# Router rows of the last mixture of experts in the padding of its shared chunks, its top-2 weights turned in 32x32 blocks on VectorE, the last norm by tiles

## The chip, the cores and the metric

The kernel runs on one core of a Trainium2 chip. Its five engines work side by side, each through its own list of instructions: TensorE (PE; PEld are its weight loads), VectorE (DVE), ScalarE (ACT), GpSimd (POOL) and SyncE (SP), which issues nearly all transfers. The metric is device time in microseconds.

## The reference

A decoder of six residual layers, each followed by a layer norm, on 1024 tokens of 256 values in float32. The first, second, third and fifth layers matter little here; the fourth (`_L1_attn_ref`) and the sixth (`_L1_ffn_ref`) are those around the change:

```python
def _L1_ffn_ref(hidden_states, gate_weight, gate_up_weights, down_weights, shared_gate_up, shared_down):
    ...
    logits = x @ gate_weight.T
    scores = jax.nn.softmax(logits, axis=-1)
    topk_w, topk_idx = jax.lax.top_k(scores, TOP_K)
    combine = jnp.zeros((T, E), x.dtype).at[jnp.arange(T)[:, None], topk_idx].add(topk_w)
    gu = jnp.einsum('th,efh->tef', x, gate_up_weights)
    act = jax.nn.silu(gu[..., :F]) * gu[..., F:]
    y = jnp.einsum('tef,te,ehf->th', act, combine, down_weights)
    sgu = x @ shared_gate_up.T
    sact = jax.nn.silu(sgu[:, :Fs]) * sgu[:, Fs:]
    y = y + sact @ shared_down.T
```
```python
    x = _layernorm(x + _L0_attn_ref(...))
    x = _layernorm(x + _L0_xattn_ref(...))
    x = _layernorm(x + _L0_ffn_ref(...))
    x = _layernorm(x + _L1_attn_ref(...))
    x = _layernorm(x + _L1_xattn_ref(x, ctx_2048, mask_BxS2_bk0))
    x = _layernorm(x + _L1_ffn_ref(...))
```

There are E = 8 experts of F = 176 rows, TOP_K = 2, and a shared expert of 352 rows.

## The kernel before

The tokens lie in eight tiles of 128, in two halves of four tiles (`HT` = 4, T0 = 0 or 4). All weights come as packs that SP loads; a pack is split into a high part (ACT) and a low part (POOL, the difference), and a product of float32 is three PE products of these parts. Feed-forward work runs in chunks s: a gate product (`g`s), an up product (`u`s), silu (`s`, ACT), their product `hraw` (`m`, DVE), its high part (`h`, ACT) and low part (`l`, POOL), and a down product (`d`, which counts packs u). The sixth layer, f1, has 14 chunks per half: 3 with the 352 shared rows padded to 384, and 11 with the experts' rows. Half 0 has the chunks 40 to 53, half 1 the chunks 54 to 67. In routed chunks DVE multiplies by the token weights (`o`), which must have been spread over the partitions.

The order of the work of each engine is written out by hand in five lists (lines 136 to 187): `SP_ORDER`, `PE_ORDER`, `ACT_ORDER`, `POOL_ORDER`, `DVE_ORDER`. An engine takes its steps in that order, whatever is ready; semaphores keep the engines in step. Names that one step has on several engines stand for parts of one thing: `G19` is a load on SP, a high part on ACT and a low part on POOL. `G16` is the first pack of f1, so `G19` belongs to the chunk of `g43`. `D`s are the down halves of packs, `S`j the four packs of the cross-attention layer (`S4` the last, split by ACT at line 1302 and by POOL at 1531). `a0.x` and `a1.x` are steps of the fourth layer's attention of half 0 and 1, with the router of f1 among them (22 to 24) although they are written as one family: for f1 of half 0 they are `a0.22` (PE `route`, line 909: 16 matmuls; DVE logits; ACT exp), `a0.23` (DVE softmax and top 2) and `a0.24` (PE four transposes, line 1075; ACT copies the weights to `cwT`, line 1380). `a1.3` and `a1.4` are queries and keys of the fourth layer's second half, `a1.5` and `a1.6` its values, `a1.7` and `a1.8` its scores (POOL subtracts the maximum there). `e`b.x are steps of the cross-attention by example, with norms before and after it (`e2.10` to `e3.12` is the norm ahead of a1). `P0` to `P3` and `Q0` to `Q3` are the token scatters and gathers of the second layer (indirect transfers, issued by POOL, lines 1461 and 1467). `w`, `x`, `y`, `z` close f1 and the last norm.

SP's list around f1 reads `... D15 R1 G16 G17 G18 G19 G20 G21 W0 C3 C4 S4 G22 C5 G23 ...`. `W0` waits until `cwT` is done, then writes it to memory; `C`k reads rows of it back, spread over the partitions, once that has landed:

```python
            def save_weights(h):
                sp.wait_ge(sems["cwT_done"], h + 1)
                sp.dma_start(cw_dram[h, :, :], cwT[0:E1, :]).then_inc(sems["cw_saved"], 16)
```

ACT's list has there `h42 S4 G19 D19 G20 D20 G21 s43`, POOL's `l42 S4 G19 D19 G20 a1.7 a1.8 l43`, PE's `a1.5 a1.6 a1.7 g43 a1.8`. `g43` waits for G19's low part (line 557 has the first matmul of a gate).

At the end, PE runs `e44 e45 e46 f44 e47 f45 f46 f47`: `e` adds the last down products to tiles 4 and 5, `f` to tiles 6 and 7. DVE's `w0` and `w1` add them to the residual by pairs of tiles and take the statistics, POOL the power, ACT (and DVE for one tile) applies the norm, SP stores by pairs.

Of the kernel before, what the change touches and what calls it, by code (L numbers as in the profile page):

```python
# [192 lines left out]
def decoder_program(nc, x_rows, x_cols, ids, pad_mask, w_attn0, w_attn1, bias_cols, bias_rows, bias_v1, bias_o,  # L193
                    w_route, temperature, consts, pk_x0, pk_f0, pk_x1, pk_f1, cw_dram, xs_dram, ys_dram, out):
    with ExitStack() as ctx:
# [344 lines left out]
        def _(pe):  # L540
# [321 lines left out]
            def down(u, tiles=range(HT)):  # L862
# [17 lines left out]
                for t in tiles:  # L880
                    o = bank[4 + t // 2][:, (t % 2) * D:(t % 2 + 1) * D]
                    if 1 <= u < U_F1 and t % 2 == 0:
                        pe.wait_ge(sems["acc_done"], 4 * u - 2 + t)
# [145 lines left out]
            def attention(i, h):  # L1029
# [38 lines left out]
                elif i == 22:  # L1068
                    route(8 + h, 1, 2 + h)
                elif i == 24:  # L1070
                    pe.wait_ge(sems["rt_cw"], h + 1)
                    if h == 0:
                        wait_x(5)
                    for t in range(HT):
# [1211 lines left out]
```

## Time and profile before

| | us |
|---|---|
| median of 3 runs | 424.13 (422.52 to 425.94) |
| the profiled execution | 422.61 |
| its span in the trace | 420.5 |

The profile is of one execution. Its page gives the busy time of each engine, the waits, the chain of work that ended last and the costliest groups of instructions; the trace gives each instruction's start and duration. Here the share of the span in which PE is busy is 96%, and its mean granted clock is 0.998 of full speed. A wait is put down to the event that came last. "L909" is line 909 of the kernel before; durations of instructions that overlap in one engine's pipeline can add up to more than the time between their starts.

### The profile page before, as it was taken

Reading aid. Unit: us, or ns where it says so; the run is one execution under the profiler, and the core shown is the slowest. Engines: PE = TensorE matmul, PEld = TensorE weight load, DVE = VectorE, ACT = ScalarE, POOL = GpSimd, SP = SyncE. Lnnn points to the kernel's source line nnn. Section 1 sums busy time; section 2 is a strip of 40 time slices with the busy share of each in tenths; the row PEclk is TensorE's granted clock in tenths of the full one; section 3 lists DMA queues with packets and bytes.
Section 4 is the critical chain, followed back from the end, with each engine's and each line's share of the span. In section 5 each row is a group of like instructions: output and inputs, shape, how many; then the busy total and the mean of one; then the engine's idle time right before and its main releaser. Section 6 shows DMA issues by size and latency. Waiting matters only on the chain.

```text
span 420.5 us, 9389 instructions
## 1 busy us (share of the span) xinstructions
PE 405.5 (96%) x3615; PEld 353.4 (84%) x3615; DVE 241.9 (58%) x647; ACT 238.8 (57%) x430; POOL 272.8 (65%) x251
## 2 busy tenths in 40 slices
PE   8999989999999999999899999999998999999993
PEld 6888979887888888888788898798687989888983
DVE  6678767627465745537554588646454675443234
ACT  4846564666667456354634867464445856553543
POOL 1754484378688775856865548477567287786863
PEclk9999999999999999999999999999999999999999
DMA  7934112443233413420502103222532241454402
GB/s 240 307 105 146 53 52 87 151 63 82 70 101 105 127 30 117 133 88 32 146 25 75 39 2 113 65 78 69 174 100 88 103 135 45 163 162 151 150 27 100
DMA packets 23239, 43.09 MB, mean 102 GB/s; under 512 B 3051, under 2 KB 10859, under 8 KB 23196
## 3 DMA queue, kind: packets, MB, share of 16 engines
q1 hardware_dynamic: 21708, 40.92, 31.1%
q0 software_dynamic: 768, 1.05, 1.3%
q8 instruction: 29, 0.48, 0.5%
q10 hardware_dynamic: 720, 0.53, 0.4%
q14 instruction: 14, 0.11, 0.1%
HBM read 38.52 MB, written 3.44 MB: 100 GB/s over the span
## 4 chain that ended last, share of the span: by engine, by line
PE 77%; POOL 6%; DVE 5%; ACT 4%; issue 4%; DMA 2%; SPq 1%; POOLq 0%; DVEq 0%
PE bank L557 13%; PE bank L558 12%; PE bank L560 12%; PE bank L890 7%; PE bank L892 7%; PE bank L891 7%; PE bank L970 2%; POOL h_lo L1510 2%; POOL x_tok L1467 2%; PE bank L958 1%; PE bank L909 1%; PE bank L580 1%; POOL xs_dram L1461 1%; PE bank L744 1%; PE bank L940 1%
## 5 line engine op out<-in xcount | busy, mean ns | idle before, releaser
L1510 POOL TENSOR_TENSOR h_lo<-hraw,h_hi 128x512 fp32r<-128x512 f32 x68 | 88.3, 1312 | 56.4 <-ACT h_hi L1260 56.2
L557 PE MATMUL bank<-xT_hi,pk_hi 128*128 128x512 f32 x240 | 97.0, 404 | 1.1 <-POOL pk_lo L1516 1.1
L558 PE MATMUL bank<-xT_hi,pk_lo 128*128 128x512 f32 x240 | 94.8, 395 | 0.7 <-issue 0.7
L1260 ACT ACTIVATE h_hi<-hraw 128x512 fp32r<-128x512 f32 x68 | 42.8, 629 | 65.1 <-DVE hraw L1909 65.1
L1516 POOL TENSOR_TENSOR pk_lo<-pk_raw,pk_hi 128x512 fp32r<-128x512 f32 (+1 forms) x44 | 74.7, 1699 | 4.0 <-ACT pk_hi L1278 3.8
L560 PE MATMUL bank<-xT_lo,pk_hi 128*128 128x512 f32 x240 | 75.5, 396 | 0.0
L1909 DVE TENSOR_TENSOR hraw<-bank,sil 128x512 f32<-128x512 f32 x68 | 46.9, 690 | 48.3 <-PE bank L560 19.3
L890 PE MATMUL bank<-pk_hi,h_hi 128*128 128x256 f32 x240 | 68.9, 287 | 1.0 <-POOL h_lo L1510 0.8
L892 PE MATMUL bank<-pk_hi,h_lo 128*128 128x256 f32 x240 | 67.8, 282 | 0.0
L891 PE MATMUL bank<-pk_lo,h_hi 128*128 128x256 f32 x240 | 67.8, 282 | 0.0
L557 PEld LDWEIGHTS bank<-xT_hi,pk_hi 128*128 128x128 f32 x240 | 45.2, 188 | 11.2 <-POOL pk_lo L1516 1.5
L560 PEld LDWEIGHTS bank<-xT_lo,pk_hi 128*128 128x128 f32 x240 | 45.1, 188 | 11.0 <-DVE xT_lo L1674 0.3
L1521 POOL TENSOR_TENSOR pk_lo<-pk_raw,pk_hi 128x256 fp32r<-128x256 f32 (+1 forms) x44 | 41.5, 943 | 19.8 <-ACT pk_hi L1289 19.7
L558 PEld LDWEIGHTS bank<-xT_hi,pk_lo 128*128 128x128 f32 x240 | 45.3, 189 | 9.7 <-issue 1.0
L890 PEld LDWEIGHTS bank<-pk_hi,h_hi 128*128 128x128 f32 x240 | 45.8, 191 | 2.7 <-issue 1.8
L891 PEld LDWEIGHTS bank<-pk_lo,h_hi 128*128 128x128 f32 x240 | 45.8, 191 | 0.8
L892 PEld LDWEIGHTS bank<-pk_hi,h_lo 128*128 128x128 f32 x240 | 45.8, 191 | 0.0
L1289 ACT ACTIVATE pk_hi<-pk_raw 128x256 fp32r<-128x256 f32 (+1 forms) x44 | 21.5, 488 | 31.2 <-PE bank L892 31.1
L1278 ACT ACTIVATE pk_hi<-pk_raw 128x512 fp32r<-128x512 f32 (+1 forms) x44 | 34.2, 777 | 8.4 <-DMA pk_raw<-pk_f_dram 4.8
L1440 POOL TENSOR_TENSOR rstd<-var_e,mhalf 128x2 f32<-128x2 f32 (+1 forms) x19 | 15.3, 808 | 28.6 <-DVE var_e L1631 28.6
L1923 DVE SCALAR_TENSOR_TENSOR x_tok<-bank,gold,x_tok 128x256 f32<-128x256 f32 x64 | 27.3, 477 | 10.9 <-PE bank L892 10.8
L1246 ACT ACTIVATE sil<-bank 128x512 f32<-128x512 f32 x46 | 27.1, 589 | 6.2 <-PE bank L560 6.1
(311 smaller groups left out, 792.8 us busy)
## 6 DMA issues: line engine op xcount, KB each, us to landing
pk_raw<-pk_f_dram SPq DMA_DIRECT2D x28, 384.0 KB, 3.2
pk_raw<-pk_f_dram SPq DMA_DIRECT2D x16, 512.0 KB, 3.7
pk_raw<-pk_f_dram SPq DMA_DIRECT2D x16, 256.0 KB, 3.2
kv_buf<-pk_x_dram SPq DMA_DIRECT2D x4, 512.0 KB, 3.5
x_tok<-x_rows_dram SPq DMA_DIRECT2D x1, 1024.0 KB, 10.3
pk_raw<-pk_x_dram SPq DMA_DIRECT2D x4, 256.0 KB, 5.9
brow<-cw_dram SPq DMA_DIRECT2D x4, 256.0 KB, 3.3
cw_late<-cw_dram SPq DMA_DIRECT2D x4, 256.0 KB, 4.1
```

What stands on the lines that cost most here:

```text
L557: pe.matmul(o, w(kc)[0], x(kc)[0], start=kc == 0, stop=False)
L558: pe.matmul(o, w(kc)[1], x(kc)[0], start=False, stop=False)
L560: m = pe.matmul(o, w(kc)[0], x(kc)[1], start=False, stop=kc == KC - 1)
L890: pe.matmul(o, hh, vh, start=first, stop=False, skip_group_check=True)
L891: pe.matmul(o, hh, vl, start=False, stop=False, skip_group_check=True)
L892: m_ = pe.matmul(o, hl, vh, start=False, stop=closed and t % 2 == 1 and kc == chunks - 1, skip_group_check=True)
L1260: A(h_hi[:, row, at * 512:(at + 1) * 512], hraw[:, s % 2, :], ACT.Copy).then_inc(sems["hid_hi"], 1)
L1278: A(g_part(kind, i, pk_hi), raw, ACT.Copy).then_inc(sems["g_hi"], 1)
L1510: pool.tensor_tensor(h_lo[:, row, q], hraw[:, s % 2, :], h_hi[:, row, q].bitcast(F32), ALU.subtract).then_inc(sems["hid_lo"], 1)
L1516: pool.tensor_tensor(g_part(kind, i, pk_lo)[:, 0:w], raw_g(kind, i)[0][:, 0:w], g_part(kind, i, pk_hi)[:, 0:w].bitcast(F32), ALU.subtract) ...
L1521: pool.tensor_tensor(d_part(kind, i, pk_lo), raw_d(kind, i)[0], d_part(kind, i, pk_hi).bitcast(F32), ALU.subtract).then_inc(sems["d_lo"], 1)
L1909: TT(hraw[:, r, :], other[:, :], sil[:, r, :], ALU.mult).then_inc(sems["hid_mul"], 1)
```

## The change

The router's eight rows of f1 go into the padding of the shared chunks (32 + 352 rows fill three packs exactly), so that the logits come out as rows 0 to 31 of the gate products of chunks 40 and 54. `route` for f1, its transposes and the copy of `cwT` are removed, with the router's share of the early weight preparation. DVE turns the logits from rows to columns with a transpose of 32x32 blocks out of PSUM into `turned` (a view of `pT`, in SBUF), takes the maximum, subtracts; ACT takes the exp; DVE divides, finds the first and second largest (`a0.23`, `a0.27`), multiplies and turns the weights back into `cwT` (`a0.28`), all on 32 partitions by 128 values. For half 0 these steps stand apart in DVE's list, `a0.28` behind `a1.5`; for half 1 they stand in a row ahead of `m54`. `SP_ORDER` is not changed.

Beside that: `l3` and `l4` go from POOL to DVE, and P0 to P3, Q0 to Q3 move against `l` steps; G16, G25, G30 and G2 stand earlier on ACT and POOL; PE takes `g40` ahead of `d19` and `g54` ahead of `d31`. The last pair of tiles is split: PE adds tile 6 (`y`) and then tile 7 (`z`, into another bank), DVE sums and takes statistics for each by itself (`w1`, `w2`), POOL takes the power of each, DVE applies the last tile's norm as (x - mean) * rstd, and SP stores each by itself.

The core of the diff:

```diff
-CH_S = -(-FS // P)
+CH_S = -(-(GS + FS) // P)
...
-e0.3 e1.3 g37 u37 g38 e0.4 e1.4 u38 e0.5 e1.5 d17 g39 u39 e0.7 e1.7 d18 a0.22 d19 g40 u40 g41 e2.12 u41 e3.12 g42
-a0.24 a1.3 a1.4 u42 d20 a1.5 a1.6 a1.7 g43 a1.8 u43 g44 u44 d21 d22 d23 a1.10 g45 a1.40 u45 a1.25 g46 a1.55 u46 a1.11
-g47 a1.41 u47 a1.26 d24 a1.56 d25 d26 d27 g48 u48 e2.2 g49 e3.2 e2.3 e3.3 u49 g50 u50 e2.4 e3.4 d28 d29 e2.5 e3.5 g51
-u51 g52 u52 d30 e2.7 e3.7 g53 u53 a1.22 d31 d32 g54 d33 u54 g55 a1.24 u55 g56 u56 g57 u57 d34 g58 d35 d36 d37 u58 g59
...
-f46 f47
...
+e0.3 e1.3 g37 u37 g38 e0.4 e1.4 u38 e0.5 e1.5 d17 g39 u39 e0.7 e1.7 d18 g40 d19 u40 g41 e2.12 u41 e3.12 g42 a1.3 a1.4
+u42 d20 a1.5 a1.6 a1.7 g43 a1.8 u43 g44 u44 d21 d22 d23 a1.10 g45 a1.40 u45 a1.25 g46 a1.55 u46 a1.11 g47 a1.41 u47
+a1.26 d24 a1.56 d25 d26 d27 g48 u48 e2.2 g49 e3.2 e2.3 e3.3 u49 g50 u50 e2.4 e3.4 d28 d29 e2.5 e3.5 g51 u51 g52 u52
+d30 e2.7 e3.7 g53 u53 g54 d31 d32 u54 d33 g55 u55 g56 u56 g57 u57 d34 g58 d35 d36 d37 u58 g59 u59 g60 u60 d38 g61 u61
...
+g62 u62 g63 d39 d40 d41 u63 g64 d42 u64 g65 u65 g66 u66 g67 u67 d43 e44 e45 e46 y44 y45 e47 y46 y47 z44 z45 z46 z47
...
-e0.2 e1.2 h34 s35 G15 h35 s36 e0.3 e1.3 e0.4 e1.4 h36 s37 h37 s38 e0.6 e1.6 h38 s39 e0.7 e1.7 D15 G16 h39 D16 G17 D17
-G18 a0.22 s40 D18 e2.11 e3.11 e2.12 e3.12 h40 a0.24 s41 S3 a1.4 h41 s42 h42 S4 G19 D19 G20 D20 G21 s43 h43 a1.9 s44
-D21 G22 D22 G23 D23 h44 s45 h45 s46 G24 h46 s47 h47 D24 G25 D25 G26 D26 e2.1 e3.1 s48 e2.2 e3.2 h48 s49 e2.3 e3.3 h49
...
+e0.2 e1.2 h34 s35 G15 h35 s36 e0.3 e1.3 e0.4 e1.4 h36 s37 h37 s38 e0.6 G16 e1.6 h38 s39 e0.7 e1.7 D15 h39 D16 G17 D17
+G18 a0.22 s40 D18 e2.11 e3.11 e2.12 e3.12 h40 s41 S3 a1.4 h41 s42 h42 S4 G19 D19 G20 D20 G21 s43 h43 a1.9 s44 D21 G22
+D22 G23 D23 h44 s45 h45 s46 G24 h46 s47 G25 h47 D24 D25 G26 D26 e2.1 e3.1 e2.2 s48 e3.2 h48 s49 e2.3 e3.3 h49 s50 e2.4
...
-p1 p3 p5 p6 p4 X0 X1 X2 X3 n0.0 G0 D0 l0 l1 n1.0 l2 P0 l3 P1 l4 P2 P3 l5 l6 l7 G1 D1 r0.0 r0.1 Q0 Q1 Q2 Q3 l8 l9 G2
-l10 D2 G3 l11 l12 r1.0 l13 D3 G4 l14 S0 l15 l16 l17 D4 G5 D5 G6 D6 l18 l19 G7 D7 l20 l21 l22 l23 G8 D8 G9 e0.10 e1.10
...
-D14 l34 G15 l35 l36 l37 e0.5 e1.5 l38 D15 l39 G16 D16 G17 D17 G18 e2.10 e3.10 l40 D18 S3 l41 l42 S4 G19 D19 G20 a1.7
-a1.8 l43 D20 G21 D21 G22 D22 G23 D23 l44 l45 e2.0 G24 l46 l47 D24 e3.0 e2.1 e3.1 G25 D25 G26 D26 l48 l49 l50 G27 D27
...
+p1 p3 p5 p6 p4 X0 X1 X2 X3 n0.0 G0 D0 l0 l1 n1.0 l2 P0 P1 P2 P3 l5 l6 l7 G1 D1 r0.0 r0.1 Q0 Q1 l8 l9 Q2 G2 Q3 l10 D2
...
+G15 l35 l36 l37 e0.5 e1.5 G16 l38 D15 l39 D16 G17 D17 G18 e2.10 e3.10 l40 D18 S3 l41 l42 S4 G19 D19 G20 a1.7 a1.8 l43
+D20 G21 D21 G22 D22 G23 D23 l44 l45 e2.0 G24 l46 G25 l47 D24 e3.0 e2.1 e3.1 D25 G26 D26 l48 l49 l50 G27 D27 G28 e2.5
+e3.5 D28 G29 D29 l51 G30 l52 D30 G31 l53 D31 G32 D32 G33 l54 l55 D33 G34 l56 l57 D34 G35 D35 G36 D36 G37 l58 D37 G38
...
-k3 m1 n1.0 m2 m3 a0 m4 m5 k4 m6 a1 m7 a2 x1.00 x1.01 a3 x1.10 x1.02 x1.11 x1.20 x1.03 x1.40 x1.12 x1.21 x1.04 x1.41
...
-m38 a17 m39 e0.7 e1.7 a18 a0.22 a19 e2.10 e3.10 a0.23 m40 e2.12 e3.12 a1.3 a1.4 m41 m42 a1.5 a1.6 a1.7 a1.8 o43 m43
-a1.9 o44 m44 a1.10 a1.25 o45 m45 o46 m46 a1.11 o47 m47 a1.26 e2.0 e3.0 o48 m48 e2.2 e3.2 e2.3 e3.3 o49 m49 o50 m50
-e2.4 e3.4 e2.5 e3.5 o51 m51 o52 m52 e2.7 e3.7 o53 m53 a1.22 a1.23 m54 x0 m55 m56 o57 m57 o58 y0 m58 o59 m59 o60 m60
-o61 m61 o62 m62 o63 m63 o64 m64 o65 m65 o66 m66 o67 m67 w0 w1 z1
...
+k3 m1 n1.0 m2 m3 a0 m4 l3 m5 l4 k4 m6 a1 m7 a2 x1.00 x1.01 a3 x1.10 x1.02 x1.11 x1.20 x1.03 x1.40 x1.12 x1.21 x1.04
...
+e1.5 m38 a17 m39 e0.7 e1.7 a18 a0.22 a19 e2.10 e3.10 m40 e2.12 e3.12 a0.23 a1.3 a1.4 m41 a0.27 m42 a1.5 a0.28 a1.6
+a1.7 a1.8 o43 m43 a1.9 o44 m44 a1.10 a1.25 o45 m45 o46 m46 a1.11 o47 m47 a1.26 e2.0 e3.0 e2.2 o48 e3.2 m48 e2.3 e3.3
+o49 m49 o50 m50 e2.4 e3.4 e2.5 e3.5 o51 m51 o52 m52 e2.7 e3.7 o53 m53 a1.22 a1.23 a1.27 a1.28 m54 x0 m55 m56 o57 m57
+o58 y0 m58 o59 m59 o60 m60 o61 m61 o62 m62 o63 m63 o64 m64 o65 m65 o66 m66 o67 m67 w0 w1 w2 z1
...
-        cwT = sb("cwT", [P, HT * P])
+        cwT = sb("cwT", [GS, HT * P])
+        turned = pT[0:GS, 0, 0:HT * P]
+        turned_e = turned.rearrange("p (b e) -> p b e", e=GS)[:, :, 0:E1]
+        most = sb("most", [GS, HT * NG])
+        prob, below = (bo1[0:GS, n * P:(n + 1) * P].rearrange("p (b e) -> p b e", e=E1) for n in range(2))
+        picked = sb("picked", [GS, HT * NG, E1])
...
-                    down(int(step[1:]), range(2) if step[0] == "e" else range(2, HT))
+                    down(int(step[1:]), {"e": (0, 1), "y": (2,), "z": (3,)}[step[0]])
...
+                elif s in (S_F1, S_F1 + N1):
+                    act.wait_ge(sems["rt_lg"], 3 + (s > S_F1))
...
-                    A(fb[:, q, :], inh[:, q, :], ACT.Exp).then_inc(sems["rt_exp1"], 1)
-                elif i == 24:
-                    act.wait_ge(sems["cwT_ps"], h + 1)
-                    if h:
-                        act.wait_ge(sems["cw_saved"], 16)
-                    A(cwT[0:E1, :], bank[7][0:E1, :], ACT.Copy).then_inc(sems["cwT_done"], 1)
+                    A(prob, below, ACT.Exp).then_inc(sems["rt_exp1"], 1)
...
+            def turned_logits(h):
+
+                s = S_F1 + N1 * h
+                dve.wait_ge(sems["gate_ready"], s + 1)
+                if h:
+                    dve.wait_ge(sems["cwT_done"], 1)
+                dve.transpose(turned, gate_bank(s)[0:GS, :]).then_inc(sems["rt_lg"], 1)
+                dve.wait_ge(sems["rt_lg"], 3 + h)
+                link(dve.tensor_reduce(most[:, :], turned_e, axis=AXX, op=ALU.max))
+                TT(below, turned_e, per_turned(most[:, :]), ALU.subtract).then_inc(sems["rt_dist"], 1)
+
+            def first_of(score):
+
+                link(dve.tensor_reduce(most[:, :], score, axis=AXX, op=ALU.max))
+                link(TT(below, score, per_turned(most[:, :]), ALU.is_equal))
+                order = from_eight.unsqueeze(1).to_broadcast([GS, HT * NG, E1])
+                link(TT(below, below, order, ALU.mult))
+                link(dve.tensor_reduce(most[:, :], below, axis=AXX, op=ALU.max))
+                return order, per_turned(most[:, :])
+
+            def turned_first(h):
+
+                dve.wait_ge(sems["rt_exp1"], h + 1)
+                link(dve.tensor_reduce(most[:, :], prob, axis=AXX, op=ALU.add))
+                link(dve.reciprocal(most[:, :], most[:, :]))
+                link(TT(prob, prob, per_turned(most[:, :]), ALU.mult))
+                link(TT(picked[:, :, :], *first_of(prob), ALU.is_equal))
+
+            def turned_second():
+
+                link(STT(turned_e, picked[:, :, :], -2.0, prob, ALU.mult, ALU.add))
+                link(TT(below, *first_of(turned_e), ALU.is_equal))
+                link(TT(picked[:, :, :], picked[:, :, :], below, ALU.add))
+
+            def turned_weights(h):
+
+                link(TT(turned_e, prob, picked[:, :, :], ALU.mult))
+                if h:
+                    dve.wait_ge(sems["cw_saved"], 16)
+                dve.transpose(cwT[:, :], turned).then_inc(sems["cwT_done"], 1)
...
+            def last_tile(t):
+
+                T = HT + t
+                dve.wait_ge(sems["sum_ps"], t + 2)
+                TT(x_tok[:, T, :], sum_part(t), x_tok[:, T, :], ALU.add).then_inc(sems["sum_added"], 1)
+                dve.wait_ge(sems["sum_added"], t + 1)
+                link(dve.bn_stats(stats[:, t, :], x_tok[:, T, :]))
+                link(dve.bn_aggr(mv[:, T, 0:2], stats[:, t, :]))
+                moments(slice(T, T + 1))
...
-                TS(x_tok[:, T, :], x_tok[:, T, :], rstd[:, T:T + 1], shift[:, T:T + 1], ALU.mult, ALU.add
+                dve.wait_ge(sems["ln_rstd"], halves_before(11) + 3)
...
+    gate[0:E1] = a["L1_ffn_gate_weight"]
+    gate[GS:GS + FS] = sgu[0:FS]
+    up[GS:GS + FS] = sgu[FS:]
+    down[GS:GS + FS] = sdn.T
```

## Rows read from the trace of the kernel before

**Rows 1.** The page's header and part 1: busy us, share, instructions.
```profile
span 420.5 us, 9389 instructions
...
PE 405.5 (96%) x3615; PEld 353.4 (84%) x3615; DVE 241.9 (58%) x647; ACT 238.8 (57%) x430; POOL 272.8 (65%) x251
```

**Rows 2.** Waits of PE, 55 to 100 and 225 to 330: total, times, longest.
```profile
PE bank L890 <- POOL h_lo L1510: 1.9, 2, 1.1
...
PE bank L557 <- POOL pk_lo L1516: 1.1, 1, 1.1
```

**Rows 3.** Timeline of POOL, 56 to 100: start, us, instruction, count, idle before.
```profile
59.77 0.96 POOL L1461 DMA_INDIRECT xs_dram<-x_tok,slot_i  x1 [0.30 <-issue]
60.76 2.53 POOL L1510 TENSOR_TENSOR h_lo<-hraw,h_hi 128x512 fp32r<-128x512 f32 x2
...
92.26 3.12 POOL L1510 TENSOR_TENSOR h_lo<-hraw,h_hi 128x512 fp32r<-128x512 f32 x2
```

**Rows 4.** The chain that ended last, in time: start, us, engine and line, count.
```profile
252.78 1.69 PE bank L909 x16
...
348.35 1.68 PE bank L909 x16
...
358.62 0.44 PE bank L1075 x4
```

**Rows 5.** Timeline of ACT, 252 to 290.
```profile
256.40 0.63 ACT L1278 ACTIVATE pk_hi<-pk_raw 128x512 fp32r<-128x512 f32 x1 [2.28 <-DMA pk_raw<-pk_f_dram]
...
266.63 0.59 ACT L1380 ACTIVATE cwT<-bank 8x512 f32<-8x512 f32 x1 [1.08 <-PE bank L1075]
...
277.42 1.04 ACT L1302 ACTIVATE xp_hi<-kv_buf 128x1024 fp32r<-128x1024 f32 x1
```

**Rows 6.** Timeline of SP's queue, 262 to 296.
```profile
268.05 0.33 SPq L489 DMA_DIRECT2D cw_dram<-cwT  x1
...
272.10 0.43 SPq L464 DMA_DIRECT2D kv_buf<-pk_x_dram  x1
```

**Rows 7.** DMA issues: times issued, size, median us to landing.
```profile
kv_buf<-pk_x_dram SPq DMA_DIRECT2D x4, 512.0 KB, 3.5
```

**Rows 8.** Timeline of POOL, 250 to 290.
```profile
254.42 1.29 POOL L1516 TENSOR_TENSOR pk_lo<-pk_raw,pk_hi 128x512 fp32r<-128x512 f32 x1
...
268.72 2.40 POOL L1531 TENSOR_TENSOR xp_lo<-kv_buf,xp_hi 128x1024 fp32r<-128x1024 f32 x1 [1.12 <-ACT xp_hi L1302]
...
278.86 2.40 POOL L1531 TENSOR_TENSOR xp_lo<-kv_buf,xp_hi 128x1024 fp32r<-128x1024 f32 x1
281.21 1.28 POOL L1516 TENSOR_TENSOR pk_lo<-pk_raw,pk_hi 128x512 fp32r<-128x512 f32 x1
```

**Rows 9.** Timeline of DVE, 252 to 290.
```profile
254.98 0.77 DVE L2133 TENSOR_TENSOR inh<-lg,s 128x32 f32<-128x32 f32 x1
...
261.33 0.19 DVE L2138 TENSOR_TENSOR fb<-fb,s 128x32 f32<-128x32 f32 x1
...
278.32 0.49 DVE L2017 TENSOR_TENSOR kv_buf<-bank,bv 128x128 f32<-128x128 f32 x2 [0.93 <-PE bank L942]
```

**Rows 10.** Groups of instructions by line, DVE: count, busy us and mean ns, idle.
```profile
L2042 DVE STREAM_TRANSPOSE pT<-sm 128x1024 f32<-128x1024 f32 x4 | 4.7, 1225 | 4.9 <-ACT sm L1371 4.9
```

**Rows 11.** The chain that ended last, at its start and from 282.
```profile
1.59 4.08 PE bank L744 x9
...
282.79 0.43 PE bank L557
283.22 0.23 PE bank L558
```

**Rows 12.** Windows: stretch and length; busy PE, PEld, DVE, ACT, POOL; clock; DMA share; GB/s.
```profile
418.00:420.00 2.00, 0.00 (x0) 0.00 (x0) 0.00 (x0) 0.00 (x0) 0.00 (x0) 0.60 0.39 131
```

**Rows 13.** The chain that ended last, its end.
```profile
414.19 0.70 DVE x_tok L2146
...
417.29 0.60 ACT x_tok L1143
```

More of the change, by code:

```diff
@@ L169 @@
+D22 G23 D23 h44 s45 h45 s46 G24 h46 s47 G25 h47 D24 D25 G26 D26 e2.1 e3.1 e2.2 s48 e3.2 h48 s49 e2.3 e3.3 h49 s50 e2.4
+e3.4 h50 G27 D27 G28 D28 G29 D29 s51 e2.6 e3.6 h51 s52 G30 e2.7 e3.7 h52 s53 D30 G31 h53 a1.22 s54 D31 G32 D32 G33 D33
+h54 s55 h55 s56 G34 h56 s57 h57 s58 D34 G35 D35 G36 D36 G37 D37 h58 s59 G38 h59 s60 D38 G39 h60 s61 h61 s62 D39 G40
+h62 s63 D40 G41 D41 h63 s64 G42 D42 G43 h64 s65 h65 s66 h66 s67 D43 h67 z0 z1
 """.split()
 POOL_ORDER = """
-p1 p3 p5 p6 p4 X0 X1 X2 X3 n0.0 G0 D0 l0 l1 n1.0 l2 P0 l3 P1 l4 P2 P3 l5 l6 l7 G1 D1 r0.0 r0.1 Q0 Q1 Q2 Q3 l8 l9 G2
@@ L880, in down @@
                 for t in tiles:
-                    o = bank[4 + t // 2][:, (t % 2) * D:(t % 2 + 1) * D]
+                    alone = u >= U_F1 + N1 and t == HT - 1
+                    o = sum_part(3) if alone else bank[4 + t // 2][:, (t % 2) * D:(t % 2 + 1) * D]
                     if 1 <= u < U_F1 and t % 2 == 0:
@@ L888, in down @@
                         vh, vl = wh[:, kc * D:(kc + 1) * D], wl[:, kc * D:(kc + 1) * D]
-                        first = fresh and kc == 0 and t % 2 == 0
+                        first = fresh and kc == 0 and (t % 2 == 0 or alone)
                         pe.matmul(o, hh, vh, start=first, stop=False, skip_group_check=True)
@@ L899, in down, with route @@
                     m_.then_inc(sems["down_done"], 1)
-            def route(n, router, m):
-                h = n % 2
-                wait_x(n)
+            def route(h):
+                wait_x(2 + h)
                 for t in range(HT):
@@ L908, in route @@
                     for j, (x, kc) in enumerate(prods):
-                        i = pe.matmul(o, x_tile(x, kc, HT * h + t), rw[:, kc, router, :, :],
+                        i = pe.matmul(o, x_tile(x, kc, HT * h + t), rw[:, kc, :, :],
                                       start=j == 0, stop=j == len(prods) - 1)
@@ L918, in golden @@
                 elif i == 3:
-                    route(2 + h, 0, h)
+                    route(h)
             def a1_project(h, j):
                 for c in range(KC):
-                    if h and j == 0 and c:
-                        pe.wait_ge(sems["cwT_done"], 1)
-                    elif j:
+                    if j:
                         pe.wait_ge(sems["a1_q"], KC * h + c + 1)
@@ L1067, in attention @@
                     a1_values(T0 + (40, 55, 41, 56).index(i), 1)
-                elif i == 22:
-                    route(8 + h, 1, 2 + h)
-                elif i == 24:
[L1071 to L1074, printed above, removed]
-                        m = pe.transpose(bank[7][0:E1, t * P:(t + 1) * P], fb[:, T0 + t, :], ident)
-                    m.then_inc(sems["cwT_ps"], 1)
             def beside(step):
@@ L1441, in rstd_of, with rstd_last @@
                 pool.tensor_tensor(shift[:, q], minus_mean[:, q], rstd[:, q], ALU.mult).then_inc(sems["ln_rstd"], 1)
+            def rstd_last(j):
+                T = HT + j + 1
+                pool.wait_ge(sems["ln_var"], halves_before(11) + 1 + j)
+                m = pool.tensor_tensor(rstd[:, T:T + 1], var_e[:, T:T + 1], mhalf[:, 0:1], ALU.pow)
+                if j == 1:
+                    link(m)
+                    m = pool.tensor_tensor(shift[:, T:T + 1], minus_mean[:, T:T + 1], rstd[:, T:T + 1], ALU.mult)
+                m.then_inc(sems["ln_rstd"], 1)
             pool.memset(zero_r[:, :].bitcast(F32), 0.0)
@@ L1501, in prepare @@
                     pool.wait_ge(sems["small_ready"], 1)
-                    link(pool.tensor_tensor(rw[:, :, :, 1, :], rw_raw[:, :, :].rearrange("p c (r e) -> p c r e", e=E0),
-                                            rw[:, :, :, 0, :].bitcast(F32), ALU.subtract))
+                    link(pool.tensor_tensor(rw[:, :, 1, :], rw_raw[:, :, :], rw[:, :, 0, :].bitcast(F32), ALU.subtract))
             def hidden_low(s):
@@ L1891, in weighted, with hidden_low @@
                 TT(sil[:, r, :], bank[2 * r][:, :], cw_all[b][:, :], ALU.mult).then_inc(sems["m1_done"], 1)
+            def hidden_low(s):
+                u, c = unit_of(s)
+                dve.wait_ge(sems["hid_hi"], s + 1)
+                row, at = place(u, c)
+                q = slice(at * 512, (at + 1) * 512)
+                TT(h_lo[:, row, q], hraw[:, s % 2, :], h_hi[:, row, q].bitcast(F32), ALU.subtract
+                   ).then_inc(sems["hid_lo"], 1)
             def hidden(s):
@@ L1981, in golden @@
                 elif i == 3:
-                    logits(h, temp[:, 1:2])
+                    logits(h)
                 elif i == 4:
@@ L2192, in _ @@
                     hidden(i)
+                elif step[0] == "l":
+                    hidden_low(i)
                 elif step[0] == "o":
```

111 lines of the change are left out of this document (53 added, 58 removed).

## The prediction

> **What bounds the kernel now.** Read the page first: TensorE (PE) is busy 405.5 of 420.5 us, no other engine over 273 [rows 1]. So a microsecond counts only where PE stands still or where a PE step goes. The waits of PE come next: POOL's hidden low parts hold it twice before 100 us, 1.9 us in all, and a low part of a weight pack holds it once, 1.1 us, at 321 [rows 2]; the other waits named in these stretches are 0.7 or less and on no step that is edited. Third, the timelines from 250 to 300 us, where most of the change lies: SP, the queue that issues the loads, carries the router weights out and back and then, behind them, the last cross-attention pack [rows 6]; ScalarE and POOL split that pack just ahead of G19 [rows 5, 8], and g43 on PE starts 0.3 us after G19's low part ends [rows 8, 11]. Here three lists are in step with about 2 us to spare.
>
> **Early reorder.** Before d2, l5 starts only at 60.76, behind the scatter P3 [rows 3]; before d4, l8 and l9 wait at 92.26 behind four gathers [rows 3]. With l3 and l4 on VectorE (DVE) and l8, l9 ahead of Q2, both waits of [rows 2] shrink, but l7, one POOL step later, then ends the wait at d3. I take -1.2 of the 1.9 (+0.75 for one more wait at d3 as the worse end, so -0.4; -1.4 the better).
>
> **Router products, first half.** Sixteen matmuls of 1.69 us and four transposes of about 0.44 go from PE [rows 4], where the second half's row stands for both halves' transposes. The logits cost nothing on PE, since the shared chunks keep three packs. But the norm that PE needs next hangs on ScalarE: G18's pack is taken at 256.40, after a wait for its landing [rows 5], and the exp, silu and the norm's apply follow in the list. PE would come early to that wait. Taken alone it gives -0.4 (0 to -2.1); it counts only if nothing later holds PE in this half, and the next part does, so it is left out of the main sum.
>
> **The weights come later, and a load with them.** Before, ScalarE's copy of the weights (266.63 + 0.59 = 267.22) releases SP's store W0 at 268.05, and 4.05 us after W0, behind the weights' way back (C3, C4), SP issues the last cross-attention pack S4 at 272.10 [rows 5, 6]. SP's list is not edited, and its wait on cwT_done blocks all that stands behind: C3, C4, S4, G22. After, cwT_done comes from a0.28, which stands behind a1.5 in DVE's list. a1.5's last value add starts at 278.32 and ends at 278.81 [rows 9]; without the transposes 0.4 earlier, 278.4. Behind it come a multiplication and a block transpose. No row has their shapes; on a line between the free 128x32 product (0.19) and the 128x1024 block transpose (1.225) [rows 9, 10], 128 elements take 0.29 and 512 take 0.69 (ends: 0.19 to 1.225 each). So cwT_done at 279.4, 12.2 us later than before. Then by rows: S4 issued 4.05 later, 283.45; landed 3.5 later [rows 7], 286.95; ScalarE's high part 1.04 [rows 5], 287.99; POOL's low part 2.40, 290.39; G19's low 1.28 [rows 8], 291.67; g43 0.3 later, 291.97 against 282.79 [rows 11]: **+9.2 bare**. Queued behind S4 on ScalarE are G19 to G21 and s43, on POOL G19, D19, G20 and the shifts of a1.7 and a1.8, on PE everything after a1.7: no cover for the 9 us.
>
> **DVE held by POOL.** The subtraction with two SBUF inputs that started at 254.98 during a POOL subtraction took 0.77 and ended 0.04 after it (254.42 + 1.29 = 255.71); the same size at 261.33, beside POOL's power, took 0.19 [rows 8, 9]. I read it as: a two-input DVE operation waits for a POOL tensor_tensor that is under way. The new steps have 11 such operations per half where 6 were. No row shows one of 32 partitions, so the ends are 0 and a full POOL operation each; I take the hold, as the row is of the same kind. Step by step: a0.23 starts after e3.12 at 265.9; l40, D18 and S3's low part (2.40 [rows 8]; it starts near 267.6, as s41 and S3 need not wait for the copy of 266.63 [rows 5]) hold it until 270.7 (bare 268.2). a1.3 on DVE, two queries of 0.75, ends at 272.2, so PE stands 2.6 us before a1.4. a0.27 starts near 277.0 and is held by l41 to 280; m42 and a1.5's adds end at 281.7; a0.28's product is held by l42 to 282.4, its transpose ends at 283.0. That is 3.6 later than bare: **+12.8** (9.2 to 14). The Trainium skill, "SBUF — State Buffer", section "Who interferes with whom", states that a VectorE instruction with two SBUF inputs contends with a GpSimd one that reads SBUF, and that the loser blocks fully, with no exception for few partitions. The trace agrees at 128 partitions [rows 8, 9]; by that rule the term is the 12.8, without it 9.2.
>
> **PE after the wait.** PE does nothing after the last matmul near 414.2, and over 418 to 420 the mean granted clock is 0.60 [rows 12]: between its two levels, so by then it had fallen from 2.4 to 1.2 GHz. The wait before g43 is 9 us or more, so PE comes back at the lower level. What that costs: when PE began at 1.59 us, nine matmuls of 512 columns took 4.08 us, against 9 x 0.23 = 2.1 for such matmuls in the middle of the span [rows 11]: **+2.0** (0 to 2.0).
>
> **G25 ahead of the residual.** G25's low part moves ahead of POOL's a1 residual and norm; the 1.1 us wait [rows 2] goes, and 0.2 of the following wait: -1.3 (0 to -1.3). G16, G30, G2 move within idle time of ScalarE and POOL: 0.
>
> **Second half.** Removed: 1.68 and 0.44 [rows 4], -2.1. DVE now runs a1.22, a1.23, a1.27, a1.28 in a row ahead of m54: 20 operations, 6.2 us bare, about 1.3 more than PE can cover if POOL's l52, D30 and G31 hold them, as m54 releases u55 and the next gates. I take -0.9 (-2.1 to 0). The weights' way out, W1, has G34 after it on SP, not a pack that is needed at once.
>
> **Tail.** The end is one chain, sum (414.19), statistics, power, apply (417.29 + 0.60), store [rows 13]. By tiles, the last tile's sum is half as wide (-0.3) and the two-input apply goes to DVE without the shift step (-0.3), but DVE first finishes tile 2 (+0.4) and the store is one more: -0.2 (0 to -0.6).
>
> **Sum.** -1.2 + 12.8 + 2.0 - 1.3 - 0.9 - 0.2 = +11.2. The profiled execution took 422.61 (span 420.5 and 2.1 around it), 1.5 below the median of the runs, 424.13; so 433.8 on its basis and 435.3 on the median's: 435.
>
> **The rivals.** *B, no hold:* operations of 32 partitions are let through; for it, that no row shows one held. -1.2 + 9.2 + 2.0 - 1.3 - 2.1 - 0.2 = +6.4, 430.5. *C, the other side, faster:* the pack is in time, the transfer hidden as before. Before, S4 lands at 275.6 and is taken at 277.42 [rows 5 to 7]: 1.8 us to spare, so it decides whether W0 goes out by 269.9. That needs a0.28 ahead of the position that its list gives it, or a pack not needed by the step behind; I find neither. Then only gains are left: -1.2 - 0.4 - 1.3 - 2.1 - 0.2 = -5.2, 418.9. *D, within 1%:* bare load, no clock cost, gains at their best: 9.2 - 1.4 - 1.3 - 2.1 - 0.6 = +3.8, 427.9.
>
> **How the numbers follow.** The forecast has 0.60. Its own range is 431 to 439: with half of the hold (11.0) and the best gains -1.4 + 11.0 + 2.0 - 1.3 - 2.1 - 0.6 = +7.6, 431.7; with 14 and the worst gains -0.4 + 14 + 2.0 = +15.6, 439.7. B has 0.18, D 0.12, C 0.10, the last kept for a mistake in reading the lists, since each link of the late load stands in the code. The range is 425 to 439: C is left out, and the upper edge. A measurement of this kernel tells about 1% (4.2 us) from no change: slower, the forecast and B, 0.78; same, D, 0.12; faster, C, 0.10.
>
> **What would show it.** In the profile after: W0 issued near 283 (B: 279.4; C: by 269.9); S4 some 4 us behind it; PE's longest wait, at L557, about 10 us, put down to POOL's pk_lo L1516; granted clock under 1.00 just behind it; a PE wait of 2 to 3 us before a1.4; DVE's new products of 32 partitions taking 0.5 to 2 us beside POOL and 0.3 elsewhere; no wait at 321 on pk_lo; no L909 rows in f1. Wrong would make it: SP going on past W0 early, or S4's halves on ScalarE and POOL passing before 280.

## The result, and the profile after

The changed kernel takes 434.15 us in the median of six runs (431.7 to 437.1), the kernel before 423.27 in six beside them (422.01 to 425.94): a ratio of 1.0259, 95% interval 1.0213 to 1.0305. That is slower, by 10.9 us against the 11.2 of the forecast. The profiled execution is the longest of the six, 437.1 us with a span of 435.2; what is read from it adds up to 14.7 us of span (435.2 less 420.5), 3.8 more than the medians tell.

The page's header and busy times of the changed kernel, which answer to [rows 1]; the last row is the granted clock in 40 slices, in tenths:

```profile
span 435.2 us, 9309 instructions
...
PE 408.0 (94%) x3575; PEld 352.8 (81%) x3575; DVE 256.6 (59%) x646; ACT 238.0 (55%) x428; POOL 270.9 (62%) x250
...
PEclk9999999999999999999999999875999999999998
```

PE has 40 matmuls less and is busier, since part of them ran at the lower clock; VectorE is busy 14.7 us longer, part of it in being held (below). Then the waits of PE from 255 to 300 us (total, times, longest), where [rows 2] had nothing above 0.7:

```profile
PE bank L566 <- POOL pk_lo L1519: 9.8, 1, 9.8
PE bank L566 <- DVE q_buf L2054: 2.6, 1, 2.6
PE bank L589 <- ACT x_tok L1131: 1.1, 1, 1.1
```

L566 is a first matmul of a gate or a projection (L557 before). The first wait is g43's, the second a1.4's, the third the norm's that the forecast named for the first half. What leads to g43, in the timelines of SP, ScalarE and POOL of the changed kernel (start, us, instruction, what ended the idle time before), which answer to [rows 5, 6, 8]:

```profile
284.03 0.30 SPq L496 DMA_DIRECT2D cw_dram<-cwT  x1
285.51 0.34 SPq L505 DMA_DIRECT2D brow<-cw_dram  x1
285.89 0.89 SPq L505 DMA_DIRECT2D cw_late<-cw_dram  x2
286.82 0.43 SPq L471 DMA_DIRECT2D kv_buf<-pk_x_dram  x1
```
```profile
291.37 1.06 ACT L1302 ACTIVATE xp_hi<-kv_buf 128x1024 fp32r<-128x1024 f32 x1 [9.61 <-DMA kv_buf<-pk_x_dram]
```
```profile
292.50 2.35 POOL L1534 TENSOR_TENSOR xp_lo<-kv_buf,xp_hi 128x1024 fp32r<-128x1024 f32 x1 [9.37 <-ACT xp_hi L1302]
294.81 1.26 POOL L1519 TENSOR_TENSOR pk_lo<-pk_raw,pk_hi 128x512 fp32r<-128x512 f32 x1
```

W0 goes out 16.0 us later than in [rows 6], S4 14.7 later; ScalarE and POOL stand more than 9 us for that one pack; G19's low part ends at 296.07, and PE's first matmul of g43 starts at 296.12, 13.4 later than before (282.72 in PE's timeline). Windows of the changed kernel from 282 to 308 (length; busy PE, PEld, DVE, ACT, POOL; the granted clock, the DMA share, GB/s):

```profile
282.00:286.00 4.00, 4.00 (x84) 3.87 (x85) 2.83 (x7) 0.00 (x0) 1.13 (x1) 1.00 0.02 4
286.00:290.00 4.00, 0.29 (x12) 0.02 (x3) 2.51 (x3) 0.00 (x0) 0.00 (x0) 0.76 0.64 224
290.00:294.00 4.00, 0.00 (x0) 0.00 (x0) 0.00 (x0) 2.63 (x6) 1.50 (x1) 0.50 0.09 38
294.00:298.00 4.00, 1.88 (x5) 1.49 (x5) 0.00 (x0) 0.59 (x2) 4.00 (x5) 0.50 0.06 18
298.00:302.00 4.00, 4.00 (x68) 2.81 (x67) 0.07 (x1) 0.58 (x1) 1.86 (x1) 0.50 0.24 84
...
304.00:308.00 4.00, 4.00 (x18) 3.29 (x17) 1.77 (x3) 2.03 (x3) 3.27 (x3) 0.86 0.18 66
```

PE falls to 1.2 GHz while it waits and stays there well into its work, until about 305.

Last, VectorE's new products of 32 partitions, and below them POOL's operations, in the two timelines. The products at 254.52, 267.07, 279.08 and 282.01 run beside the four POOL operations, in this order; the one at 277.84 has no POOL operation beside it, and the last row is the block transpose:

```profile
254.52 1.30 DVE L1960 TENSOR_TENSOR bo<-pT,most 32x128 f32<-32x128 f32 x1
...
267.07 2.34 DVE L1967 TENSOR_TENSOR bo<-bo,con 32x128 f32<-32x128 f32 x1
...
277.84 0.28 DVE L1965 TENSOR_TENSOR bo<-pT,most 32x128 f32<-32x128 f32 x1
...
279.08 1.28 DVE L1983 TENSOR_TENSOR picked<-picked,bo 32x128 f32<-32x128 f32 x1
...
282.01 1.26 DVE L1987 TENSOR_TENSOR pT<-bo,picked 32x128 f32<-32x128 f32 x1
283.30 0.70 DVE L1990 STREAM_TRANSPOSE cwT<-pT 32x512 f32<-32x512 f32 x1
```
```profile
254.38 1.29 POOL L1519 TENSOR_TENSOR pk_lo<-pk_raw,pk_hi 128x512 fp32r<-128x512 f32 x1
...
266.85 2.42 POOL L1534 TENSOR_TENSOR xp_lo<-kv_buf,xp_hi 128x1024 fp32r<-128x1024 f32 x1
...
278.94 1.28 POOL L1513 TENSOR_TENSOR h_lo<-hraw,h_hi 128x512 fp32r<-128x512 f32 x1 [9.67 <-ACT h_hi L1260]
...
281.84 1.29 POOL L1513 TENSOR_TENSOR h_lo<-hraw,h_hi 128x512 fp32r<-128x512 f32 x1 [1.61 <-ACT h_hi L1260]
```

Each of the four ends 0.14 or 0.15 us after the POOL operation beside it (267.07 + 2.34 = 269.41 against 266.85 + 2.42 = 269.27); alone such a product takes 0.28.

### The profile page after: what moved, and what is told of

Its sections match the earlier page's. It is cut to its first block, busy times and chain, and to the rows that moved or that the text cites. A ratio compares the mean times of both kernels' runs of the same rounds, so it can differ in the third digit from the quotient of the medians.

```text
span 435.2 us, 9309 instructions
## 1 busy us (share of the span) xinstructions
PE 408.0 (94%) x3575; PEld 352.8 (81%) x3575; DVE 256.6 (59%) x646; ACT 238.0 (55%) x428; POOL 270.9 (62%) x250
## 4 chain that ended last, share of the span: by engine, by line
PE 71%; DVE 8%; ACT 7%; issue 6%; POOL 4%; DMA 3%; SPq 0%; POOLq 0%; DVEq 0%; ACTq 0%
PE bank L566 13%; PE bank L567 12%; PE bank L569 12%; PE bank L900 6%; PE bank L902 5%; PE bank L901 5%; PE bank L977 2%; PE bank L965 1%; DVE hraw L1923 1%; ACT sil L1246 1%; DMA q_buf<-x_cols_dram 1%; PE bank L589 1%; DMA kv_buf<-pk_x_dram 1%; ACT x_tok L1141 1%; ACT L1246 1%
## 5 line engine op out<-in xcount | busy, mean ns | idle before, releaser
L1513 POOL TENSOR_TENSOR h_lo<-hraw,h_hi 128x512 fp32r<-128x512 f32 x66 | 86.1, 1316 | 63.3 <-ACT h_hi L1260 63.0
L566 PE MATMUL bank<-xT_hi,pk_hi 128*128 128x512 f32 x240 | 98.4, 410 | 10.7 <-POOL pk_lo L1519 10.0
L567 PE MATMUL bank<-xT_hi,pk_lo 128*128 128x512 f32 x240 | 95.8, 399 | 1.5 <-issue 1.5
L569 PE MATMUL bank<-xT_lo,pk_hi 128*128 128x512 f32 x240 | 76.4, 400 | 0.0
L566 PEld LDWEIGHTS bank<-xT_hi,pk_hi 128*128 128x128 f32 x240 | 45.9, 191 | 22.8 <-POOL pk_lo L1519 10.6
L569 PEld LDWEIGHTS bank<-xT_lo,pk_hi 128*128 128x128 f32 x240 | 45.7, 190 | 11.2 <-DVE xT_lo L1680 0.3
```

Source lines behind the costliest of these rows:

```text
L566: pe.matmul(o, w(kc)[0], x(kc)[0], start=kc == 0, stop=False)
L567: pe.matmul(o, w(kc)[1], x(kc)[0], start=False, stop=False)
L569: m = pe.matmul(o, w(kc)[0], x(kc)[1], start=False, stop=kc == KC - 1)
L1513: pool.tensor_tensor(h_lo[:, row, q], hraw[:, s % 2, :], h_hi[:, row, q].bitcast(F32), ALU.subtract).then_inc(sems["hid_lo"], 1)
```

## The experiments

All times are medians, all ratios against the kernel before beside them, with their 95% intervals. The theory L is that of the forecast: the pack S4, behind W0 on SP, holds ScalarE, POOL and so PE; VectorE's hold by POOL makes it later still; PE restarts at half speed.

**The load ahead of the store** (`SP_ORDER` of the changed kernel):

```diff
-... G20 G21 W0 C3 C4 S4 G22 ...
+... G20 G21 S4 W0 C3 C4 G22 ...
```

> The changed kernel, only SP's list: S4 (load of the last cross-attention pack) ahead of W0. Theory L (the late pack is most of the loss): the 9.8 us wait before g43 and the slow restart behind it go; PE reaches g43 near 286.3, 3.5 after before's 282.8, and what is left is the wait before a1.4 (2.6 us and its slow restart, 1.5): about 424, ratio to before 0.995 to 1.01. Rival H (VectorE held by POOL, not the pack, sets the time): S4's place changes little, 430 to 434. Rival N (some other of the edits slowed the kernel): 428 to 434 without any wait at g43.

Measured: 422.68 us, 1.0014 (0.9993 to 1.0035). One exchange in a list takes back nearly all of the loss (2.6% to 0.1%). PE's waits from 255 to 300 now:

```profile
PE bank L566 <- DVE q_buf L2054: 2.6, 1, 2.6
PE bank L589 <- ACT x_tok L1131: 1.1, 1, 1.1
```

g43's wait is gone, a1.4's is what it was, although W0 itself still goes out late, at 282.34. So the loss came from what stood behind the store, not from the weights. H and N fall as main causes.

**Queries ahead of a0.23** (`DVE_ORDER` of the changed kernel), alone and with S4 first:

```diff
-... e3.12 a0.23 a1.3 a1.4 m41 ...
+... e3.12 a1.3 a0.23 a1.4 m41 ...
```

> The changed kernel, only VectorE's list: a1.3 (queries) ahead of a0.23, so that the steps held by POOL no longer stand before what PE needs for a1.4; the pack still comes behind W0. Theory L with the hold as its second term: the 2.6 us wait before a1.4 and its slow restart (1.5) go, W0 goes out near 280 instead of 284, g43 near 292 instead of 296: 430, ratio 1.012 to 1.02. If the hold costs nothing on PE's path: 433 to 435. If the hold is the main cause: 424 to 426.

> Both edits at once: S4 ahead of W0 in SP's list, a1.3 ahead of a0.23 in VectorE's. Theory L with the hold as second term: all that is left are the gains, 418 to 420, ratio 0.988 to 0.993. If a third cause of some microseconds is left in the change: 422 to 426.

Measured: alone 431.74, 1.0209 (1.0172 to 1.0247); with S4 first 421.67, 0.9973 (0.9953 to 0.9993). The wait before a1.4 is gone in both. Alone it gives 2.4 us by the medians where 4 were expected, and the intervals overlap with the changed kernel's; a new wait of 1.7 us appears in a1.6 (VectorE adds the values late). With both, 1.7 to 3.7 us are still missing to the 418 to 420 of the gains: a third cause was open.

**S3's low part out of the way of a0.23** (`POOL_ORDER` of the changed kernel; no VectorE step moves):

```diff
-... l40 D18 S3 l41 l42 S4 ...
+... l40 D18 l41 l42 S3 S4 ...
```

> The changed kernel, only POOL's list: the low part of S3 (2.4 us) goes from ahead of l41 to behind l42, so that it no longer runs beside a0.23; VectorE's and SP's lists are as in the changed kernel. If a two-input VectorE operation is held by a POOL tensor_tensor: the third product of a0.23 falls from 2.34 us to 0.28, a0.23 ends near 268.3 instead of 270.1, PE's wait before a1.4 shrinks from 2.6 us to 1 or less with no slow restart behind it, W0 goes out 2 to 3 us earlier: 430.5 to 432. If something else made those operations long: no change, 433.5 to 435.

Measured: 430.97, 1.0192 (1.0138 to 1.0245), 3.2 us less than the changed kernel by the medians, though the intervals overlap. W0 goes out at 279.13, 4.9 us earlier where 2 to 3 were expected. The rows are clearer than the time. In VectorE's timeline of this kernel the product that had taken 2.34, and in the waits of PE that before a1.4:

```profile
266.65 0.28 DVE L1967 TENSOR_TENSOR bo<-bo,con 32x128 f32<-32x128 f32 x1
```
```profile
PE bank L566 <- DVE q_buf L2054: 0.6, 1, 0.6
```

What made it long was the POOL operation beside it. That the hold reaches operations of 32 partitions is shown.

**PE kept at work in the wait** (gate 43 of the changed kernel; `zero_r` holds zeros, `o` is the bank that g43 overwrites, `FILL` is 38):

```diff
+                    if s == S_F1 + 3:
+                        pe.wait_ge(sems["silu_done"], s - 1)
+                        for _ in range(FILL):
+                            pe.matmul(o, zero_r[:, 0:P], zero_r[:, :], start=True, stop=True)
                     pe.wait_ge(sems["g_lo"], 2 * E0 + u - U_F1 + 1)
```

> The changed kernel with 38 matmuls of zeros (512 columns, into the bank that g43 overwrites) on PE just ahead of its wait for G19's low part, so that PE works through most of the 9.8 us. They are extra work of 8.9 us inside the wait and leave the result as it is. If the slow restart behind the wait costs 2 to 4 us, the granted clock stays at 1.00 from 286 to 306 and the kernel gets 2 to 4 us faster: 430 to 432. If the clock is not what costs there: 434 or a little more.

Measured: 432.67, 1.0244 (1.0181 to 1.0307): 1.5 below the changed kernel, but the intervals overlap, so the time decides nothing. In its windows the clock does what was expected:

```profile
290.00:294.00 4.00, 4.00 (x19) 3.34 (x18) 0.00 (x0) 2.56 (x5) 1.42 (x1) 1.00 0.08 29
294.00:298.00 4.00, 3.54 (x20) 2.35 (x22) 0.00 (x0) 0.71 (x3) 4.00 (x4) 1.00 0.01 3
298.00:302.00 4.00, 4.00 (x75) 3.34 (x71) 2.40 (x3) 0.55 (x1) 2.04 (x2) 1.00 0.28 95
```

And the traces decide what the restart costs. PE's timelines show the first matmul of g43 and the first of the down products behind it, in the changed kernel and then in this one (whose lines stand one or five further down):

```profile
296.12 0.80 PE L566 MATMUL bank<-xT_hi,pk_hi 128*128 128x512 f32 x1 [9.84 <-POOL pk_lo L1519]
307.57 0.28 PE L900 MATMUL bank<-pk_hi,h_hi 128*128 128x256 f32 x1
```
```profile
296.28 0.50 PE L567 MATMUL bank<-xT_hi,pk_hi 128*128 128x512 f32 x1 [0.46 <-POOL pk_lo L1524]
303.67 0.28 PE L905 MATMUL bank<-pk_hi,h_hi 128*128 128x256 f32 x1
```

g43 starts at the same time, but the same work takes 7.39 us instead of 11.45, and 7.39 is what it takes in the kernel before (282.72 to 290.11). So in these executions the low clock behind the wait costs 4.1 us.

**a0.28 behind a1.6, and m54 ahead of a1.27** (with S4 first and the queries first):

```diff
-... a0.27 m42 a1.5 a0.28 a1.6 a1.7 ...
+... a0.27 m42 a1.5 a1.6 a0.28 a1.7 ...
-... a1.22 a1.23 a1.27 a1.28 m54 x0 ...
+... a1.22 a1.23 m54 a1.27 a1.28 x0 ...
```

> S4 ahead of W0, a1.3 ahead of a0.23, and a0.28 behind a1.6 instead of between a1.5 and a1.6. If the 1.7 us wait that is left in a1.6 (VectorE adds the values behind a held a0.28) costs its size: 1 to 1.7 us below the kernel with the first two edits (421.7), 420 to 420.7. If the weights then come too late for o43, or the wait only moves: 421.5 to 422.5.

> As the one before, and in the second half m54 ahead of a1.27 and a1.28. If the run of 20 VectorE operations ahead of m54 takes back 1.3 of the 2.1 us that the removed PE work gives in the second half: 0.8 to 1.3 us less than without it. If PE has the cover for it: no difference.

Measured: the first line alone 421.94, 0.9965 (0.994 to 0.999); both 422.04, 0.9979 (0.9953 to 1.0006). Neither moves the time; the gains that they were made for did not come. The 1.7 us wait in a1.6 stays, so a0.28 does not make the values late. What is left ahead of them is a0.27, ahead of m42, of which one product runs from 274.88 to 276.21 beside l41; the next experiment but one moves it, with a0.23 and a0.28, and the wait is gone. In the second half m54 comes earlier, but the weights later, and then VectorE waits for them (timeline of the kernel with both lines):

```profile
274.88 1.33 DVE L1967 TENSOR_TENSOR bo<-bo,con 32x128 f32<-32x128 f32 x1
...
366.56 0.69 DVE L1897 TENSOR_TENSOR sil<-bank,cw_late 128x512 f32<-128x512 f32 x1 [1.96 <-DMA cw_late<-cw_dram]
```

**The early reorder alone** (kernel before; the orders of l3, l4, P, Q and G2, h10 as in the change):

```diff
-... l2 P0 l3 P1 l4 P2 P3 l5 ... Q0 Q1 Q2 Q3 l8 l9 G2 l10 ...
+... l2 P0 P1 P2 P3 l5 ... Q0 Q1 l8 l9 Q2 G2 Q3 l10 ...
```

> The kernel before with the early reorder alone: l3 and l4 on VectorE, P0 to P3 together, l8 and l9 ahead of Q2, h10 behind G2. By the trace of the changed kernel the work of PE from its first hidden product to chunk 20 is 1.4 us shorter: 1.2 to 1.5 us faster than before, ratio 0.9965 to 0.997. If what is gained there is lost again at a later wait: 0.999 to 1.001.

Measured: 421.86, 0.9963 (0.9936 to 0.999): 0.9 us by the medians, 0.4 to 2.7 by the interval. In the trace PE is 1.4 earlier up to chunk 20, and part of it goes at later waits.

**VectorE's steps where it is idle**, with S4 first, and the same without:

```diff
-... m40 e2.12 e3.12 a0.23 a1.3 a1.4 m41 a0.27 m42 a1.5 a0.28 a1.6 ...
+... m40 a0.23 e2.12 e3.12 a1.3 a0.27 a1.4 m41 a0.28 m42 a1.5 a1.6 ...
```

> S4 ahead of W0, and the first half's router steps on VectorE where it is idle and POOL mostly is too: a0.23 behind m40 (VectorE stands 2.2 us there for the norm), a0.27 between a1.3 and a1.4, a0.28 behind m41. If what is left of the loss in this half are the waits for VectorE in a1.4 to a1.6 (0.6 and 1.7 us with the earlier edits): 1.5 to 2.3 us below them, 419.5 to 420.5, ratio 0.991 to 0.995. If the waits move on to another step: 421.5 to 422.5.

> The same places on VectorE, but SP's list as in the changed kernel, W0 ahead of S4: a middle dose of the late load. W0 goes out near 275 instead of 284; S4 issued near 278, landed near 282.3, g43 near 287.4. By theory L the wait before g43 is 4 to 5 us instead of 9.8, with a slow restart behind it: 425 to 429. If the load's lateness were not what counts: as the one before, 419.5 to 421.

Measured: with S4 first 419.19, 0.9903 (0.9878 to 0.9929), the fastest of all and 1% below the kernel before; with SP's list as in the change 426.93, 1.0111 (1.0067 to 1.0156). Here is the third cause: the places of a0.23, a0.27 and a0.28, 2.5 us (421.67 to 419.19, and the intervals are apart; 2.3 in the spans of the two traces). The 1.7 us wait in a1.6 is gone. The product of a0.23 that took 2.34 takes 0.28 here, at 262.34, where POOL does nothing. The two runs differ by one exchange on SP. In the second, W0 goes out at 275.94, and the longest wait of PE is

```profile
PE bank L566 <- POOL pk_lo L1519: 5.9, 1, 5.9
```

A W0 that is 8.1 us earlier than in the changed kernel lets g43 start 8.1 us earlier (288.04 instead of 296.12). The wait is only 3.9 shorter, since PE comes to it 4.2 earlier as well. The load follows the store one to one. Between the two kernels lie 7.7 us by the medians and 6.8 by the spans of their traces: 5.5 at g43's start (282.49 with S4 first), and 1.3 in the slow restart behind it, where the stretch from g43 to the down products takes 8.66 instead of 7.39.

**x0 behind m55** (added to the fastest):

```diff
-... m54 x0 m55 m56 ...
+... m54 m55 x0 m56 ...
```

> As the first of this group, and in the second half x0 (1.3 us of VectorE, the first half's sum) behind m55 instead of ahead of it. The wait for hraw that is left there is 0.7 us: 0.4 to 0.7 us faster if nothing else ends that wait, no difference if the sum is then late for the first down product of the second half.

Measured: 419.47, 0.9907 (0.9878 to 0.9936). No difference; the wait for hraw is still 0.7.

**All of the change without the router:**

```diff
-... l38 D15 l39 G16 D16 ... G24 l46 l47 D24 e3.0 e2.1 e3.1 G25 ...
+... G16 l38 D15 l39 D16 ... G24 l46 G25 l47 D24 e3.0 e2.1 e3.1 ...
-... e44 e45 e46 f44 e47 f45 f46 f47
+... e44 e45 e46 y44 y45 e47 y46 y47 z44 z45 z46 z47
```

(the lists of POOL and PE; with the early reorder, the lists of ScalarE and VectorE to match and the functions for the last tiles from the change; `route` and the copy of `cwT` are as before.)

> All of the change but its name: the kernel before with the early reorder, the earlier places of G16, G25, G30 and the last norm by tiles; the router of f1 stays as before (products and transposes on PE, weights of 128 partitions, W0 released by ScalarE). By the traces: early -0.9 to -1.4, G25 -1.1 or nothing, the tail -0.7: 420 to 421, ratio 0.993 to 0.996. Then the moved router, at its best places and with S4 first (419.2), brings 1 to 2 us by itself. If it comes out at 419 or less, the moved router brings nothing even there; at 422 or more, the other edits don't add up.

Measured: 419.5, 0.9931 (0.9904 to 0.9958). The side edits are worth 0.7%. Against the fastest kernel's 0.9903 the intervals overlap, the medians are 0.3 us apart, and the spans of the two traces are 417.1 here and 417.3 there: that the moved router brings anything, even at its best places, is not shown.

## Why the prediction was right, step by step

The forecast of 435 (range 425 to 439) and its way hold: the late load behind W0, with the hold, is the loss. By the profiled execution of the changed kernel its terms came out so; one of them, the restart, was mis-sized.

- **The late load and the hold**, +12.8. W0 at 284.03 (forecast 283.0), g43 at 296.12 (295.6), PE's wait there 9.8, "about 10". (These forecast times leave out what the early reorder gains; with the 0.8 us that PE is ahead at 253, g43 would be at 294.8.) From 253 to 296 us PE loses 14.2 against before; 1.6 of that is the slow restart at a1.4 (below), 12.6 the term. Two of its parts were wrong in opposite directions, and that they nearly cancel is luck: from W0 to S4 it took 2.8, not 4.05 (the store of the weights came back in 1.5 instead of 2.7), and S4 took 4.55 to land, not 3.5.
- **The hold** was the likelier of two readings of one row at 128 partitions; the rows above and the moved S3 decide it for 32. The Trainium skill, "SBUF — State Buffer", section "Who interferes with whom", has a VectorE instruction with two SBUF inputs contend with a GpSimd one that reads SBUF, over ports that one of them holds alone: the trace agrees (2.34 beside POOL, 0.28 alone), and reductions with one input keep their 0.27. Not every POOL operation holds, though: in the kernel before, a product of 128x32 took 0.19 at 261.33 while POOL's power of 128x2 ran from 261.07 to 261.77. Rival B, without the hold, would have been 430.5; the kernel with S3 moved, 430.97, is about that, though its smaller holds are left and the low clock behind g43 lasts 9 us there.
- **PE after the wait**, +2.0, was too small for this execution, by two mistakes. First, a restart was counted once: the 2.6 us wait before a1.4 was in the sum, but PE came out of it at 0.50 as well, with eight matmuls of 512 columns 0.43 apart instead of 0.23, 1.6 us. Second, the price came from the kernel's start, where the slow matmuls were over after 4 us (they are 0.43 us apart, as at the lower level, though the windows there give the clock as 1.00). Behind g43 the clock was low for 9 us, until about 305: from g43 to the down products behind it the loss grows from 13.40 to 17.46, 4.1 us. In the kernel with the queries first it was low for 3.4 us, from 293.0 to 296.4 (windows below), and the same work took 1.5 us more than in the kernel before. So the term is 1.3 to 4.1 us in these traces.
- **G25**, -1.3: the wait at 321 on pk_lo has no successor, and from those down products to the x1 scores the loss falls from 17.46 to 16.05, -1.4.
- **Second half**, -0.9: 16.05 to 15.38, -0.7. The hold is there too: two-input products of 0.65 to 0.96 beside POOL, and 0.28 alone, ahead of m54, and a wait of 0.7 for hraw behind it.
- **Tail**, -0.2: the way from PE's last matmul to the last store's issue is shorter by that (3.5 instead of 3.8 us), but the last store is one tile instead of two and ends 0.4 sooner. Together -0.7: the size of the store was left out of the term.
- **Early reorder**, -1.2: 1.5 in this trace, of which 0.4 is given back by chunk 40; 0.9 by time when alone.
- **C**, faster, needed W0 by 269.9; **D** needed the load without the hold and no price for the clock. Neither came.

The sum by the trace: +0.3 (a later start) - 1.5 + 0.4 + 14.2 + 4.1 - 1.4 - 0.7 - 0.7 = +14.7. The forecast had 11.2 in its place, with one restart at 2.0 where this trace has two, 1.6 and 4.1. The medians' 10.9 is 3.8 less than the trace, and the clock is a likely reason: the mean clock of the six runs is 0.972 to 0.984, lowest in the profiled one, the longest. By estimate from mean clock and span, the clock was low for 24 us there and for 14 to 17 us in the other five, and 7 to 10 us less at half speed are 3.5 to 5 us. So that the forecast lies 0.3 us from the medians is partly luck: what one restart costs differs by more than that.

## What to carry to other kernels

When a producer moves to a later place, look up what stands behind the wait for it in every in-order queue, not only who reads the result: here the weights themselves were in time, and the load behind their store cost 11 us. Place a VectorE step with two SBUF inputs by what POOL does at that time, not only by what VectorE has free. A wait of PE of some microseconds costs its own length and, behind it, a slow restart: here 1.3 to 4.1 us behind waits of 2.6 to 9.8.

## What was unexpected of the hardware

After a wait of 2.6 us PE came out at 1.2 GHz: in the changed kernel the clock is 1.00 from 268 to 270, while PE waits for a1.3's queries, then 0.75, 0.50 and 0.90 in the next three stretches of 2 us, 3.4 us at the lower level. How long the clock stays low once PE works again, from the windows in which it rises (at 0.86 over 304 to 308 it was 0.50 for 1.1 of the 4 us, so until 305.1), did not grow in step with the wait. The last column is the time from g43's first matmul to the first down product behind it:

| kernel | wait before g43 | low clock behind it | g43 to down products |
|---|---|---|---|
| before | none | none | 7.39 |
| PE kept at work | 0.5 | none | 7.39 |
| idle places, W0 first | 5.9 | 2.9 | 8.66 |
| queries first | 8.5 | 3.4 | 8.91 |
| S3 moved | 8.7 | 9.0 | 11.42 |
| changed | 9.8 | 9.0 | 11.45 |

Windows of the kernel with the queries first, whose g43 starts at 292.99:

```profile
288.00:292.00 4.00, 0.00 (x0) 0.00 (x0) 0.00 (x0) 3.23 (x6) 2.62 (x2) 0.50 0.00 0
292.00:296.00 4.00, 3.01 (x10) 1.97 (x14) 0.00 (x0) 0.04 (x1) 4.00 (x4) 0.50 0.31 97
296.00:300.00 4.00, 4.00 (x74) 3.36 (x71) 2.15 (x3) 0.54 (x1) 0.74 (x1) 0.95 0.02 5
```

What decides it stays open: no run here varied it by itself.
